# Attention heads of a mixture-of-experts block: TensorE in six stretches per head, the exponentials' scale in a register, the turned sums through ScalarE, VectorE and GpSimd

## What is computed

```python
q, k, v = (qkv[:, :, 0], qkv[:, :, 1], qkv[:, :, 2])
attn = jnp.einsum('bqhd,bkhd->bhqk', q, k) / jnp.sqrt(jnp.asarray(hd, x.dtype))
attn = jax.nn.softmax(attn, axis=-1)
attn_out = jnp.einsum('bhqk,bkhd->bqhd', attn, v).reshape(B, S, D)
...
moe_out = jnp.einsum('bsef,bse->bsf', expert_out, combine)
return attn_out + moe_out
```

## Time and profile before

| | |
|---|---|
| median of the runs shown | 3701.96 us |
| span of the profiled execution | 3704.9 us |
| TensorE, VectorE, ScalarE, GpSimd busy | 93%, 88%, 70%, 48% |
| the second phase's first exponential starts at | 1903.7 us |
| exponentials | 2048, 702 ns each |
| row maxima | 1024, 1216 ns each |

### The profile page before, as it was taken

One profiled execution on the slowest core, in us unless ns is written; L12 is line 12 of the kernel. 1 busy time (PEld: TensorE's weight loads), 2 busy tenths in 40 slices (PEclk: granted clock), 3 DMA queues, 4 the chain that ended last, 5 costly groups with the idle time before them and its releaser, 6 DMA issues.

```text
span 3704.9 us, 119843 instructions
## 1 busy us (share of the span) xinstructions
PE 3461.2 (93%) x52062; PEld 1579.2 (43%) x52062; DVE 3253.8 (88%) x3103; ACT 2586.1 (70%) x3896; POOL 1784.5 (48%) x1563
## 2 busy tenths in 40 slices
PE   6999999999999999999599999999999999999997
PEld 3545555555545545555332323324233242332422
DVE  6899989989988998998699797997979979799796
ACT  4665757666565766656359597695976959769598
POOL 5787878878887887878231210312103121031210
PEclk8999999999999999999799999999999999999999
DMA  4444535444444444435350602406024060250600
GB/s 116 127 126 109 147 101 137 122 127 123 108 136 109 135 115 124 127 99 143 86 79 2 92 25 36 80 2 92 25 38 78 2 92 25 36 80 2 92 13 13
DMA packets 145232, 307.76 MB, mean 83 GB/s; under 512 B 24484, under 2 KB 64068, under 8 KB 144452
## 3 DMA queue, kind: packets, MB, share of 16 engines
q1 hardware_dynamic: 144708, 300.10, 35.7%
HBM read 230.68 MB, written 35.13 MB: 72 GB/s over the span
## 4 chain that ended last, share of the span: by engine, by line
PE 17%; ACT 12%; issue 11%; DVE 10%; DMA 0%; ACTq 0%; SPq 0%; DVEq 0%; POOL 0%
ACT probs L1575 12%; PE ps L1362 6%; PE ps L1347 4%; DVE neg_max L1689 3%; PE ps L1397 2%; PE ps L1464 2%; PE ps L1377 1%; PE ps L1409 1%; DVE acc L1841 1%; PE ps L1308 1%; DVE att L1748 1%; DVE acc L1829 1%; DVE acc L1774 1%; DVE x1T L1671 1%; DVE x1T L1669 1%
## 5 line engine op out<-in xcount | busy, mean ns | idle before, releaser
L353 POOL TENSOR_TENSOR z<-z,c_rep 128x1024 f32<-128x1024 f32 x512 | 1412.9, 2771 | 333.8 <-DVE z L891 325.4
L1575 ACT ACTIVATE probs<-ps,e_scale 128x512 f32<-128x512 f32 x2048 | 1242.4, 702 | 113.4 <-PE ps L1347 111.0
L891 DVE TENSOR_TENSOR_SCAN z<-dA,ps 128x1024 f32<-128x1024 f32 x512 | 1157.9, 2278 | 135.2 <-PE ps L411 90.0
L1689 DVE TENSOR_REDUCE neg_max<-ps 128x1 f32<-128x1024 f32 x1024 | 1187.4, 1216 | 42.4 <-PE ps L1308 41.4
L729 ACT ACTIVATE dA<-rep,a_rep 128x1024 f32<-128x1024 f32 x512 | 565.7, 1142 | 222.4 <-DVE z L891 219.2
L411 PEld LDWEIGHTS ps<-diag,u_t 64*64 64x64 f32 x32768 | 532.2, 135 | 391.7 <-issue 391.4
L1347 PE MATMUL ps<-q_st,k_st 50*128 50x512 f16 x2048 | 631.8, 383 | 32.1 <-ACT probs L1575 28.6
L411 PE MATMUL ps<-diag,u_t 64*64 64x64 f32 x32768 | 599.5, 222 | 61.8 <-DVE z L891 42.6
L1362 PE MATMUL ps<-probs,v_h 128*32 128x256 f32 x8192 | 647.7, 390 | 0.6 <-ACT o_sb L1582 0.6
L1308 PE MATMUL ps<-k_st,q_st 48*128 48x512 f16 x2048 | 598.9, 383 | 7.8 <-DVE neg_max L1689 6.9
L430 PE MATMUL ps<-z,eye 128*64 128x512 f32 x2048 | 507.1, 616 | 0.9 <-issue 0.9
(11 more groups left out here) (190 smaller groups left out, 3096.4 us busy)
## 6 DMA issues: line engine op xcount, KB each, us to landing
c_rep<-c_scratch SPq DMA_DIRECT2D x512, 256.0 KB, 4.0
rep<-delta SPq DMA_DIRECT2D x128, 256.0 KB, 4.4
q_st<-qk_halves SPq DMA_DIRECT2D x192, 128.0 KB, 10.0
k_st<-qk_halves SPq DMA_DIRECT2D x192, 128.0 KB, 10.6
qk_halves<-qk_parts SPq DMA_DIRECT2D x32, 512.0 KB, 10.7
x_nat<-in_x SPq DMA_DIRECT2D x9, 1024.0 KB, 7.9
x_rows<-x_nat SPq DMA_DIRECT2D x9, 1024.0 KB, 7.0
xT<-in_xT SPq DMA_DIRECT2D x8, 1024.0 KB, 7.3
```

The source lines that it names most:

```text
L353: pool.tensor_tensor(z[:, k % ZR, :], z[:, k % ZR, :], c_rep[:, slot, :], ALU.mult).then_inc(s_zc, 1)
L891: dve.tensor_tensor_scan(z[:, k % ZR, :], dA[:, k % AR, :], pair(1 + k % 2), 0.0, ALU.mult, ALU.add).then_inc(s_z, 1)
L1575: act.activation(probs[:, kt, half * HALF:(half + 1) * HALF], ps[:, ring_bank(("probs", h, 2 * kt + half)), :], ACT.Exp, scale=e_scale[:, ...
L1689: dve.tensor_reduce(neg_max[:, h % 2, qt:qt + 1], pair(qt % 2), AX.X, ALU.max, negate=True).then_inc(s_mx, 1)
```

## The change

- On TensorE the units and the key tiles are no longer interleaved as 2 units and 1 tile, eight times. A table STRETCHES gives six blocks of units, (0, 1, 2), (3, 4, 5), (6, 7), (8, 9, 10), (11, 12), (13, 14, 15), followed by 1, 1, 2, 1, 1 and 2 tiles of `weigh_v`. The `scores` matmuls stay beside their units, so that the two matmuls of query tiles 1, 5 and 6 stand in different blocks.
- The exponential's scale comes from one of 16 registers of ScalarE, loaded once from `e_scale`.
- `take_max` on ScalarE moves from behind unit 8 to behind unit 7.
- The turned sums are copied to SBUF by ScalarE (`take_sums`, after unit 12), inverted by VectorE (`invert_sums`, after its query tile 7 instead of 5) and multiplied by GpSimd (`normalise`, at the end of its step). TensorE waits for the copy and no longer for the product before it reuses the bank.

```diff
-        r_sum = sb("r_sum", [P, 2, QUARTERS, 1])
+        r_sum = sb("r_sum", [P, 2, 2, QUARTERS, 1])
+        o_nat = sb("o_nat", [P, 2, 2, QUARTERS, HD + 1])
...
+        STRETCHES = ((0, 3, 1), (3, 6, 1), (6, 8, 2), (8, 11, 1), (11, 13, 1), (13, 16, 2))
...
+                def normalise(h):
+                    g = b * HEADS + h
+                    to = att[:, :, h * HD:(h + 1) * HD].rearrange("p (j i) c -> p i j c", i=2)
+                    if h == 0:
+                        pool.wait_ge(s_done, (b + 1) * 16)
+                    pool.wait_ge(s_rc, g + 2)
+                    pool.tensor_tensor(to, o_nat[:, h % 2, :, :, 0:HD],
+                                       r_sum[:, h % 2, :, :, :].broadcast_to([P, 2, QUARTERS, HD]), ALU.mult).then_inc(s_nm, 1)
...
+            def sums_read(b, h):
+
+                pe.wait_ge(s_on, b * HEADS + h + 2)
...
-                for kt in range(TT):
-                    for half in range(2):
-                        scores_t(b, h, kt, half)
+                weighed = 0
+                for first, last, tiles in STRETCHES:
+                    for i in range(first, last):
+                        scores_t(b, h, i // 2, i % 2)
                         if ahead:
-                            scores(b, h + PRE, kt, 1 - half)
-                    if before and kt < LAG:
-                        weigh_v(b, h - 1, TT - LAG + kt)
...
+                            scores(b, h + PRE, i // 2, 1 - i % 2)
+                    for kt in range(weighed, weighed + tiles):
+                        if before and kt < LAG:
+                            weigh_v(b, h - 1, TT - LAG + kt)
+                        if kt >= LAG:
+                            weigh_v(b, h, kt - LAG)
+                        if h == 0 and kt in (0, 2):
+                            expert(b, LAST + kt // 2)
+                        if turned and kt == 3:
+                            turn_max(b, h + 1)
+                        if before and kt == 5:
+                            turn_o(b, h - 1)
+                        for work, args in front.get(kt, ()):
+                            work(b + 1, *args)
+                    weighed += tiles
...
-                               scale=e_scale[:, h:h + 1]).then_inc(s_p, 1)
+                               scale=head_scale[h]).then_inc(s_p, 1)
...
+            def take_sums(b, h):
+                g = b * HEADS + h
+                act.wait_ge(s_ot, g + 2)
+                act.wait_ge(s_nm, g)
+                act.activation(o_nat[:, h % 2, :, :, :], turned_sums(h)[:, :, :, 0:HD + 1], ACT.Copy).then_inc(s_on, 1)
...
-                        if turned and kt == 4 and half == 0:
+                        if turned and kt == 3 and half == 1:
                             take_max(b, h + 1)
+                        if before and kt == 6 and half == 0:
+                            take_sums(b, h - 1)
...
+            act.wait_ge(s_hsc, 1)
+            act.load(head_scale, e_scale[0:1, :].bitcast(mybir.dt.int32))
...
-            def normalise(b, h):
+            def invert_sums(b, h):
                 g = b * HEADS + h
...
-                dve.wait_ge(s_ot, g + 2)
-                dve.reciprocal(r_sum[:, :, :, :], o[:, :, :, HD:HD + 1]).then_inc(s_rc, 1)
-                dve.wait_ge(s_rc, g + 1)
-                dve.tensor_tensor(to, o[:, :, :, 0:HD], r_sum[:, :, :, :].broadcast_to([P, 2, QUARTERS, HD]),
-                                  ALU.mult).then_inc(s_nm, 1)
+                dve.wait_ge(s_nm, g)
+                dve.wait_ge(s_on, g + 2)
+                dve.reciprocal(r_sum[:, h % 2, :, :, :], o_nat[:, h % 2, :, :, HD:HD + 1]).then_inc(s_rc, 1)
...
-                    if qt == 5 and before:
-                        normalise(b, h - 1)
+                    if qt == 7 and before:
+                        invert_sums(b, h - 1)
```

More of the change, by code:

```diff
@@ L1066, in attention_phase @@
         s_qr = sem("qk_scale_chain")
+        s_hsc = sem("head_scales_ready")
         s_bt = sem("qk_bias_turned")
@@ L1120, in attention_phase @@
         s_nm = sem("head_normalised")
+        s_on = sem("turned_sums_taken")
         s_at = sem("attention_added")
@@ L1157, in ring_bank, with turned_sums @@
             return RING[SLOT[user] % 3] if user in SLOT else 7
+        def turned_sums(h):
+            return ps[:, ring_bank(("sums", h, 0)), 0:2 * P].rearrange("p (i j c) -> p i j c", i=2, c=VC)
         block = ctx.enter_context(nc.Block())
@@ L1243, in _ @@
             pool.sem_inc(s_pv, TT)
+            pool.sem_inc(s_nm, 1)
             pool.sem_inc(s_pa, 4)
@@ L1294, in _ @@
                         add_scaled(LAST // 2)
+                    else:
+                        normalise(h - 1)
+                normalise(HEADS - 1)
         @block.tensor
@@ L1329, in ring_free @@
                     else:
-                        pe.wait_ge(s_nm, b * HEADS + h + 2)
+                        sums_read(b, h)
             def turn_max(b, h):
@@ L1336, in turn_max @@
                 else:
-                    pe.wait_ge(s_nm, b * HEADS + 1)
+                    sums_read(b, -1)
                 pe.wait_ge(s_mp, (b * HEADS + h + 1) * 2)
@@ L1373, in turn_o @@
                 else:
-                    pe.wait_ge(s_nm, g + 1)
+                    sums_read(b, h - 1)
                     pe.wait_ge(s_p, (g + 1) * (2 * TT) + 2)
@@ L1547, in _ @@
             act.sem_inc(s_o, 1)
+            act.sem_inc(s_on, 1)
+            head_scale = [act.alloc_register(f"head_scale{h}") for h in range(HEADS)]
             act.preload_act_table(ACT.Ln)
@@ L1616, in heads @@
                 take_o(b, HEADS - 1)
+                take_sums(b, HEADS - 1)
             def inv_std(b):
@@ L1663, in _ @@
             dve.sem_inc(s_ot, 1)
-            dve.sem_inc(s_nm, 1)
+            dve.sem_inc(s_rc, 1)
             dve.wait_ge(s_wq, 16 * 3)
@@ L1733, in heads @@
                     split_qk(b + 1, 0)
-                normalise(b, HEADS - 3)
+                invert_sums(b, HEADS - 3)
                 if more:
@@ L1737, in heads @@
                         split_qk(b + 1, mt)
-                normalise(b, HEADS - 2)
+                invert_sums(b, HEADS - 2)
                 if more:
@@ L1741, in heads @@
                         take_v(b + 1, t)
-                normalise(b, HEADS - 1)
+                invert_sums(b, HEADS - 1)
             def add_experts(b, first, last):
@@ L1897, in _ @@
             dve.wait_ge(s_qs, 16)
-            dve.tensor_scalar(e_scale[:, :], e_scale[:, :], HD ** -0.5 / Q_UP ** 2, None, ALU.mult)
+            dve.tensor_scalar(e_scale[:, :], e_scale[:, :], HD ** -0.5 / Q_UP ** 2, None, ALU.mult).then_inc(s_hsc, 1)
             dve.wait_ge(s_w, WEIGHTS)
```

## The result

The changed kernel takes 3782.7 us (median, 3775.4 to 3784.2) against 3702.3: a ratio of 1.0209, interval 1.0194 to 1.0223 (four executions of each; the 3701.96 given for the kernel before is the median of the first three). It is slower by 2.1%; the prediction said 3776.

A forecast was written before the change was run, and what follows sets the result against it. Three engines nearly full, joined by bank pairs and ring; split tiles lengthen the head from 9.94 to 10.54 us. 104 full steps +62, step 0 +10, rest small: total +74, span 3779, median 3776; range 3722 to 3812.

The forecast's parts named there:

- The links: Delays between starts of VectorE's query-tile maxima, through TensorE's queue and bank pairs; summed to a head of 10.54 us.
- maximum 7 to 1: From query tile 7's maximum start to the next head's tile 1: 2.61 us, against 2.46 for VectorE alone.
- 1 to 4: From tile 1's maximum start to tile 4's, with two weighing tiles and turned maxima between: 3.73 us; VectorE alone 3.39.
- 4 to 6: From tile 4's maximum start to tile 6's, across a weighing tile and `turn_o`: 2.98 us; VectorE alone 2.26.
- 6 to 7: From tile 6's maximum start to tile 7's on VectorE: 1.13 us.
- the late exponential 10: TensorE's unit 12 also needs exponential 10, seen 1.36 instead of 1.27 after maximum 4's start; head 10.54, not 10.45.
- The sums: Work per head without waits: TensorE 8.96 us (9.4 before), ScalarE 8.3, VectorE 9.2, the largest.
- The joints hold: Rival: VectorE never starved, head 9.2 us, 104 x -0.7 = -73, time 3629; chance 0.10.
- Only the splits bind: Rival: link from maximum 1 to 4 shrinks to VectorE's 3.39, head 10.11, time 3726; chance 0.12.
- The register saves nothing: Rival: exponential keeps pitch 0.58 and duration 0.69, head 10.83, time 3808; chance 0.15.
- step 0: First step of each sequence: `scale_expert` and turned maxima come later, VectorE waits longer; +1.3 us each, 8 x 1.3 = +10.
- Steps 14 and 15: Steps without maxima at a sequence's end: about +0.5 in 7 sequences, +3; in the last sequence 2 back.

The follow-up runs named there:

- the column scale: Changed kernel with the exponential's scale taken from an SBUF column again instead of a register: head 10.83 us, 3818.1 us, ratio 1.0298.
- the halved readers: Changed kernel with maxima over 512 of 1024 keys and exponentials over 256 of 512 columns: blocks head 9.27, 3591.7 us; with eight rounds 9.45, 3602.8 us.
- the rounds: Changed kernel set back to eight rounds of two units and one tile, maxima over 512 of 1024 keys: head 9.66 us, 3629.3 us.
- the halved maxima: Changed kernel, blocks kept, each VectorE maximum over 512 of 1024 keys: head 9.99 us, 3672.0 us.

## Why the prediction was right

**The links.** They are the argument, and each can be read off VectorE's rows above:

| link | predicted | measured |
|---|---|---|
| maximum 7 to 1 | 2.61 | 2.61 (2444.11 to 2446.72) |
| 1 to 4 | 3.73 | 3.71 |
| 4 to 6 | 2.98 + 0.09 | 3.09 |
| 6 to 7 | 1.13 | 1.14 (2442.97 to 2444.11) |
| head | 10.54 | 10.55 |

(Maximum 7 stands inside a merged row; taken alone it starts at 2444.11.) The 0.09, the late exponential 10, was tested by the column scale: 10.83 was forecast for it, 10.83 measured.

**The sums.** VectorE's 9.2 and TensorE's 8.96 for blocks would have misled as a forecast; the halved readers bear out TensorE's (9.05 without unit 14's wait). The exponential's price, 0.48 of pitch and 0.60 of duration, came out at 0.48 to 0.49 and 0.60. GpSimd's product was taken at 0.45 and took 0.40; one wait for it, of 0.5 us, is in the whole trace. ScalarE was to be idle for some 2 us per head; the window above has 2.84 in 20 us, 1.5 per head.

**The rivals.** "The joints hold" needed less than 2.26 from a maximum to the one two on, and the links across the splits measured 2.61 and 3.09. "Only the splits bind" needed 3.39 for the second link, which measured 3.71; that rival's head of 10.11 also left out the 0.09 of exponential 10, and with it would have been 10.20. "The register saves nothing" is out by the exponential's 597 ns.

**What was off.** The terms outside heads 2 to 13 were off by up to 4.5 us each, and that they nearly cancel is luck. Added up over the sequences, heads 2 to 13 took 58.3 us more (forecast 57.6), step 0 5.5 (10), step 1 8.1 (4.8), steps 14 and 15 1.0 less (1 more), and the stretches between sequences 1.8 more (1): 72.7 against 74. Step 0 was counted at +1.3 and grew by 0.8 (12.73 to 13.53, the change in most of the eight sequences); the expert product that moves behind units 6 and 7 is the last one, not the second last as the prediction has it. Step 1, counted as a full step with +0.6, grew by 1.1 (9.98 to 11.09), perhaps since it inherits what step 0 leaves. Steps 14 and 15 were counted at +0.5 together and did not change (16.69 and 13.56) in sequences 0 to 6. In the last sequence 1.0 came back, not 2. I also listed a wait before maximum 5; there is none, because maximum 4 is itself late and 5 follows it without one (by 1.18).

**What was incomplete.** The prediction blamed the splits. The runs show two causes that lie over one another: the split tiles, and the blocks of three against the ring of three. With the maxima's wait taken away, 0.56 of the blocks' loss goes (10.55 to 9.99), and they are still 0.33 behind the rounds. Unit 5's wait, 0.27 there, does not show in the changed kernel, where the `scores` matmuls beside units 2 and 4 are late already (2445.38, 2446.58) and exponential 2 is done by then; the prediction did not name it, and the expectation for the halved maxima did.

## What to carry to other kernels

A longer run of one kind of work on one engine saves that engine's switches and asks more buffers of its readers: before grouping, take every pair of producers that a reader needs together and follow the shortest loop through its buffer, from the reader's start to its start two on, with everything queued in between. If that loop is longer than the reader's own two steps, the saving is lost, whatever the three engines' sums say. And change one thing at a time: here the register was worth 1.3%, and the rest of the edit took away more than that.

## What the runs showed of the hardware

- An exponential whose scale comes from a register is cheaper than one whose scale is a column of SBUF: 512 columns take 597 ns (median) instead of 688, and back to back they follow each other at 477 or 494 ns instead of 570 or 586. No run has this exponential with a constant scale.
- The Trainium skill, "ScalarE: Activation LUTs", What ACT_TABLE_LOAD costs, gives about 93 ns for a pointer operand; the difference of the shortest pitches is 93 (570 and 477).
- A weighing tile right behind another costs 0.43 us inside a head too: 16 of its matmuls take 1.07 (at 2448.54 in the changed kernel) where 8 take 0.64.
- TensorE's busy share says little about waits below 0.2 us: it is 98% with 0.5 us of waits in a head of 9.94 (sum 9.42) and 96% with 1.6 us in a head of 10.55 (sum 8.96).
